# Base rows written in place by ScalarE, x and bias added to them by accumulating DMAs, most of them behind the return of the attention rows

## The reference, cut to what matters

```
x = x + gnn(xn, edges) + mix(xn)          # first residual
x = x + ffn(layernorm(x))                 # second residual, FP4-rounded weights and rows
gnn: rms scale, W_down (1024 to 256), xl = x@Wl, xr = x@Wr, per edge a LeakyReLU score,
     a softmax over the edges of each receiver, sum of alpha * xl[src], then @ W_up (256 to 1024)
mix: q, k, v = xn@W + b;  (q k^T) v * scale;  @Wo + bo      # no softmax in it
ffn: gate, up (1024 to 512), silu(gate) * up, down (512 to 1024)
```

## Time and profile before

| | us |
|---|---|
| median of 3 runs | 917.87 (916.38 to 919.6) |
| the profiled execution, its own time | 920.16 |
| its span, first to last instruction | 918.4 |
| PE busy | 856.0 (93%) |
| DVE busy | 817.6 (89%) |
| ACT busy | 549.5 (60%) |
| POOL busy | 498.9 (54%) |
| mean granted TensorE clock | 0.968 of full speed |

### The profile page before, as it was taken

The page is one execution under the profiler, slowest core; times in us unless marked ns, Lnnn a source line. Parts: engine busy times, 40 slices in busy tenths (PEclk is TensorE's granted clock), DMA queues, the critical chain, the costliest instruction groups (busy, mean ns, idle before and its releaser), DMA issues.

```text
span 918.4 us, 9530 instructions
## 1 busy us (share of the span) xinstructions
PE 856.0 (93%) x2734; PEld 417.5 (45%) x2734; DVE 817.6 (89%) x987; ACT 549.5 (60%) x1947; POOL 498.9 (54%) x528
## 2 busy tenths in 40 slices
PE   4999999999999999999999999997999699999665
PEld 3885455644444444444444444432444244444222
DVE  7989988779999999999999999999994277999994
ACT  3313123356767887779898988798995332353432
POOL 5200748578667777777777787877775200010011
PEclk9999999999999999999999999997999899999877
DMA  9322625563655333663345633349959911113125
GB/s 306 98 95 52 179 85 178 143 196 99 84 162 184 97 89 89 193 202 107 102 122 172 193 97 100 91 111 190 382 111 204 207 49 46 69 24 69 24 46 87
DMA packets 72403, 117.85 MB, mean 128 GB/s; under 512 B 29383, under 2 KB 42340, under 8 KB 72330
## 3 DMA queue, kind: packets, MB, share of 16 engines
q0 software_dynamic: 27520, 63.68, 30.2%
q1 hardware_dynamic: 44826, 53.52, 18.6%
HBM read 89.15 MB, written 17.17 MB: 116 GB/s over the span
## 4 chain that ended last, share of the span: by engine, by line
DVE 61%; PE 14%; issue 9%; POOL 8%; DMA 6%; ACT 1%; ACTq 0%; SPq 0%; POOLq 0%; DVEq 0%
DVE acc_sb L1487 12%; DVE turned L1479 11%; DVE z L1639 11%; DVE turned L1637 10%; PE acc L745 3%; POOL round_mem L550 3%; PE turned L900 2%; DMA round_mem<-msg_table,idx 2%; PE acc L933 2%; DMA acc_sb<-gnn_dram 2%; PE acc L900 2%; PE turned L955 1%; POOL round_mem L628 1%; POOL perm_dram L599 1%; POOL xr_sb L632 1%
## 5 line engine op out<-in xcount | busy, mean ns | idle before, releaser
L550 POOL DMA_INDIRECT round_mem<-msg_table,idx x352 | 345.5, 982 | 99.5 <-issue 80.0
L1122 ACT ACTIVATE round_mem<-round_mem,pz 128x65 f32<-128x65 f32 x1408 | 354.1, 398 | 7.0 <-DVE acc_sb L1487 3.0
L745 PE MATMUL acc<-wslot,big_a 128*128 128x512 f32 x512 | 220.3, 592 | 0.0
L745 PEld LDWEIGHTS acc<-wslot,big_a 128*128 128x128 f32 x512 | 97.1, 190 | 121.5 <-issue 121.3
L1487 DVE TENSOR_REDUCE acc_sb<-round_mem 128x260 f32<-128x1820 f32 (+1 forms) x62 | 121.6, 1962 | 7.2 <-ACT round_mem L1122 5.1
L1479 DVE TENSOR_TENSOR turned<-round_mem,turned 128x1560 f32<-128x1560 f32 (+1 forms) x62 | 105.4, 1700 | 7.4 <-DMA round_mem<-msg_table,idx 5.4
L1112 ACT ACTIVATE pz<-z 128x7 f32<-128x7 f32 (+1 forms) x248 | 55.4, 296 | 93.7 <-DVE z L1644 93.6
L745 PE MATMUL acc<-big_b,wslot 128*128 128x512 f32 x256 | 110.1, 592 | 0.2 <-ACT big_b L1058 0.2
L745 PE MATMUL acc<-wslot,big_b 128*128 128x512 f32 x256 | 110.0, 592 | 0.0
L1639 DVE TENSOR_REDUCE z<-turned 128x24 f32<-128x1560 f32 (+1 forms) x62 | 105.1, 1695 | 2.1
L1637 DVE SCALAR_TENSOR_TENSOR turned<-turned,att_sb 128x1536 f32<-128x1536 f32 (+1 forms) x62 | 103.6, 1671 | 0.0
(11 more groups left out here) (231 smaller groups left out, 1045.4 us busy)
## 6 DMA issues: line engine op xcount, KB each, us to landing
round_mem<-msg_table,idx POOLq DMA_INDIRECT x352, 2.8
big_b<-in_x SPq DMA_DIRECT2D x9, 512.0 KB, 7.7
big_b<-big_b SPq DMA_DIRECT2D x9, 512.0 KB, 13.2
big_b<-in_x POOLq DMA_DIRECT2D x9, 512.0 KB, 12.8
out_x<-big_b SPq DMA_DIRECT2D x9, 512.0 KB, 3.2
out_x<-acc_sb POOLq DMA_DIRECT2D x9, 512.0 KB, 5.4
wslot<-in_wv_t SPq DMA_DIRECT2D x2, 2048.0 KB, 9.3
wslot<-in_wk_t SPq DMA_DIRECT2D x2, 2048.0 KB, 9.5
```

What stands on the lines that cost most here:

```text
L550: pool.indirect_dma_start(xg[g % 4][:, j, :], None, msg_table, bass.IndirectOffsetOnAxis(idx[:, c, j0 + j:j0 + j + 1], 0)).then_inc(xg_in[ ...
L745: mm = nc.tensor.matmul(o(acc[:, n % 4, :]), a, b, start=first, stop=last)
L1122: ins = nc.scalar.activation(to[:, :, j], xg[g % 4][:, j, h * HR + 1:(h + 1) * HR], ACT.Copy, scale=pz[:, g % 2, j, h:h + 1])
```

## The change

The early base products are no longer laid aside. ACT copies each half straight from PSUM into the rows of the residual, and POOL then adds x and the bias row to them with accumulating DMAs. The order of the products is (0,0), (1,0), (0,1), (1,1), then (2,0), (2,1) and so on as before. For chunks 6 to 8, SP reads x straight into the rows, and only the bias is added. Of the sixteen accumulating DMAs, six (x of chunks 0 to 2, bias of 0 to 2) stand between POOL's last three rescalings, and ten (x of 3 to 5, bias of 3 to 8, x of 9) stand behind a wait for `gnn_in[1]`. Since x of chunk 9 is added to the place in which the bias row lies, it waits for all nine bias additions.

```diff
-BIAS_SUMS_AT, X_AT = 40, 61
+BIAS_SUMS_AT, AHEAD = 40, 3
+BETWEEN = {-2: {"x": (0, 1, 2), "bias": ()}, -1: {"x": (), "bias": (0, 1)}, 0: {"x": (), "bias": (2,)}}
...
-         "base": [(c, h) for c in range(EARLY) for h in range(2)]}
+         "base": [(c, h) for h in range(2) for c in range(2)] + [(c, h) for c in range(2, EARLY) for h in range(2)]}
...
-            sp.wait_ge(acc_taken["dve"], taken[index_of["bias", 1]])
-            for c in range(C - 1):
-                sp.dma_start(base[:, c, :], bias_bc).then_inc(x_in[c], 16)
+            sp.wait_ge(acc_full, index_of["bias", 1] + 1)
+            for c in range(EARLY, C - 1):
+                sp.dma_start(base[:, c, :], x[c * NC:(c + 1) * NC, :]).then_inc(x_in[c], 16)
...
             def add_x(c):
                 n = rows(c)
-                if c < C - 1:
-                    pool.wait_ge(x_in[c], 32)
+                if c < EARLY:
+                    pool.wait_ge(acc_taken["act"], taken[index_of["base", ORDER["base"].index((c, 1))]])
                 else:
                     for i in range(C - 1):
-                        pool.wait_ge(x_in[i], 32)
-                pool.dma_start(base[0:n, c, :], x[c * NC:c * NC + n, :], accum_op=ALU.add).then_inc(x_added[c], 16)
-
-            def lay_base(c):
-                pool.wait_ge(acc_taken["act"], taken[index_of["base", ORDER["base"].index((c, 1))]])
-                pool.wait_ge(x_added[c], 16)
-                pool.dma_start(base[:, c, :].rearrange("p (k n) -> p k n", k=KB), base_at[c], accum_op=ALU.add).then_inc(base_added[c], 16)
+                        pool.wait_ge(bias_added[i], 16)
+                pool.dma_start(base[0:n, c, :], x[c * NC:c * NC + n, :], accum_op=ALU.add).then_inc(x_added[min(c, EARLY)], 16)
+
+            def add_bias(c):
+                if c < EARLY:
+                    pool.wait_ge(x_added[c], 16)
+                else:
+                    pool.wait_ge(x_in[c], 32)
+                pool.wait_ge(acc_taken["dve"], taken[index_of["bias", 1]])
+                pool.dma_start(base[:, c, :], bias_bc, accum_op=ALU.add).then_inc(bias_added[c], 16)
...
-                if X_AT <= g < X_AT + C - 1:
-                    add_x(g - X_AT)
             for g in range(LAST - 2, LAST + 1):
+                for c in BETWEEN[g - LAST]["x"]:
+                    add_x(c)
+                for c in BETWEEN[g - LAST]["bias"]:
+                    add_bias(c)
                 rescale(g)
-                if g == LAST - 2:
-                    for c in range(max(LAST + 1 - X_AT, 0), C):
-                        add_x(c)
             for c in range(C):
                 if LAST_OF[c] + 5 > LAST:
                     send_attention(c)
-            for c in range(EARLY):
-                lay_base(c)
+            pool.wait_ge(gnn_in[1], 16)
+            for c in range(AHEAD, EARLY):
+                add_x(c)
+            for c in range(AHEAD, C - 1):
+                add_bias(c)
+            add_x(C - 1)
...
                 elif kind == "base":
                     c, h = ORDER["base"][i]
-                    act.wait_ge(acc_full, index_of["base", ORDER["base"].index((c, 1))] + 1)
-                    nc.scalar.copy(base_at[c][:, 4 * h:4 * h + 4, :], a.rearrange("p (k n) -> p k n", k=4)).then_inc(t, 1)
+                    nc.scalar.copy(base[:, c, h * HALF:(h + 1) * HALF], a).then_inc(t, 1)
...
             def residual(c, h):
-                    if c < EARLY:
-                        dve.wait_ge(base_added[c], 16)
+                    if c < C - 1:
+                        dve.wait_ge(bias_added[c], 16)
                     else:
-                        dve.wait_ge(x_added[c], 16)
+                        dve.wait_ge(x_added[EARLY], 16)
```

More of the change, by code:

```diff
@@ L223, in gps_layer @@
         x_in = [sem(f"x_in{c}") for c in range(C)]
-        x_added = [sem(f"x_added{c}") for c in range(C)]
-        base_added = [sem(f"base_added{c}") for c in range(EARLY)]
+        x_added = [sem(f"x_added{c}") for c in (*range(EARLY), C - 1)]
+        bias_added = [sem(f"bias_added{c}") for c in range(C - 1)]
         wd_in, rms_in, wlr_in = sem("wd_in"), sem("rms_in"), sem("wlr_in")
@@ L299, in gps_layer @@
                for i in range(2)]
-        base_at = [xhat_t[:, :, c * NC:(c + 1) * NC] for c in range(C)]
         gnn_tr = xr_sb[:, :, :].rearrange("p c f -> p (c f)")[:, 0:2 * NP].rearrange("p (k n) -> p k n", k=2)
@@ L883, in _ @@
                 c, h = ORDER["base"][i]
-                if i in (0, 1):
+                if i in (0, 2):
                     pe.wait_ge(acc_taken["act"], taken[index_of["t2", 7 if i == 0 else 15]])
@@ L985, in gps_layer @@
                 round_of[n], at = g, full
-                if kind == "base" and ORDER["base"][i][1] == 1:
-                    round_of[index_of["base", ORDER["base"].index((ORDER["base"][i][0], 0))]] = g
                 begun += TAKE_STEP if engine == "dve" else 0.0
@@ L993, in gps_layer @@
         for n in range(n, len(groups)):
-            kind, i, _ = groups[n]
             round_of[n] = LAST + 1
-            if kind == "base" and ORDER["base"][i][1] == 1:
-                round_of[index_of["base", ORDER["base"].index((ORDER["base"][i][0], 0))]] = LAST + 1
         def due(engine, g):
@@ L1614, in sum_p0 @@
                 ins.then_inc(p0_summed, 1)
-            assert round_of[index_of["bias", 1]] + 3 < X_AT
             def sum_bias(k):
```

## The result

The changed kernel took 933.98 us (median of 4 runs, 933.21 to 934.01). The kernel before took 918.15 us in 4 runs (916.38 to 919.6). The ratio is 1.0177, with a 95% interval of 1.0158 to 1.0196: the change makes the kernel 1.8% slower, 15.8 us. The forecast was 933 us. The profiled execution has a span of 931.7 us (before 918.4) and took 933.97 us itself, so the two profiled executions are only 13.8 us apart, because the profiled execution of before (920.16 us) was slower than all four of these. In the sixth and the seventh experiment one execution (1833.37 and 929.76 us) stood far off from the others: it is in their medians, not in their ratios.

A forecast was written before the change was run, and what follows sets the result against it. Rounds end on DVE and ACT, queued accumulations stretch the return, then PE is the chain. Root 13.1 us later plus 1.8 us of clock gives +14.9 us, the return's 12.3 spent on waiting: 933 us, range 926 to 939.

The forecast's parts named there:

- ACT's copies: In the rounds: twelve same-size copies, one at a time instead of in pairs, hidden behind DVE; 0, bounds -1 and +1 us.
- SP's bias copies: In the rounds: nine bias copies become three copies of x; at most 0.45 us to be had, value 0.
- the six early additions: Between POOL's last rescalings: their waits end before DVE needs the rescaling; value 0, with 2.6 us of cover.
- The return: Second reading-back of attention rows after the last sending: lands in 5.5 us, at 714.5 instead of 726.8, 12.3 us earlier.
- The ten additions: On POOL behind the return: chunk 0's root waits for all nine biases and ends at 743.8, 13.1 us later.
- The disputed price: Cost of each queued bias addition behind the return: taken as 2.48 us, bounds 1.31 and 2.90.
- The rivals with a cheaper bias: Additions behind the return at plain-copy pace: bias only, about 926 us (12 in 100); all accumulations, about 922 (6 in 100).
- the quoted rule: Trainium skill's DMA estimate, 1.2 us per further 512 KB: root ends about 731.3, sum near +3 us, time about 921.
- The chain through ACT to PE: At the tail's head: late root delays ACT's normalising and attention rows 6 and 7; PE starts 4.4 us after root's end.
- The clock: PE after its idle time, inside its first tail matmuls: lower clock loses 1.8 us, bounds 0 and 4.
- Nothing behind gives time back: In the tail after PE's delayed start: the chain has no fixed date, so nothing of the 14.9 us is recovered.
- last rival: At POOL's first root: if ready with ACT's deviation, the early return moves everything up some 10 us, about 908 (4 in 100).

The follow-up runs named there:

- sixth: The kernel with roots between the additions (908.2 us), but without POOL's wait for the return: 911.74 us, ratio 0.9941 to the kernel before.
- seventh experiment: The changed kernel with all ten additions behind the return, and POOL's wait for it, left out: 907.21 us, ratio 0.9882 to the kernel before.
- fifth experiment: The changed kernel without the bias additions for chunks 6, 7 and 8: 925.6 us, ratio 1.0088 to the kernel before.
- first two experiments: Changed kernel with x of chunk 9 added behind three roots: 919.76 us; changed kernel with ACT taking attention rows 6 and 7 before normalising chunk 0: 926.36 us.
- first experiment: The changed kernel with x of chunk 9, and its wait for nine biases, behind POOL's first three roots: 919.76 us, ratio 1.0022.
- third experiment: The changed kernel with roots of chunks 0 and 1 between the bias additions and x of chunk 9 behind the third root: 908.22 us, ratio 0.9893.
- fourth experiment: The changed kernel without POOL's wait for the return, x of chunks 3 and 4 issued right behind the sending: 931.15 us, ratio 1.015.

## Why the prediction was right

The forecast was 933 us with a range of 926 to 939, measured 933.98. Its steps, between the two profiled executions:

- *ACT's copies, SP's bias copies, the six early additions (0).* From DVE's first sum of the rounds to its last, 501.1 us before and 500.4 now, so 0.7 us were won, within the bounds of 1 us. I did not separate by whom. The rounds also began 0.7 us earlier (200.4 instead of 201.1), so that the last sending started 1.4 us earlier, at 704.00. The rescaling of round 60 ended at 691.15, ahead of DVE's need at 693.90.
- *The return (12.3 us earlier).* Against the last sending it is 8.46 us (704.00 to 712.46) instead of 21.4: 12.9 us earlier. The sending landed in 2.5 instead of the 3.2 I took, the reading-back in 5.5 as taken.
- *The ten additions (the root 13.1 us later).* From the last sending to the root's end it is 39.1 us now, and it was 25.3 before: 13.8 us later. The disputed price, 2.48 us for a bias addition, was right: the fifth experiment gave 2.48 again. The last of them land within 1.38 MB of traffic at 94.1% of the 16 engines. The rivals with a cheaper bias are out, and with them what the quoted rule gave for the end of the root (731.3).
- *The chain through ACT to PE.* Right. PE began L906 4.0 us behind the root's end (4.4 before), and the first two experiments cut the chain at both ends.
- *The clock (1.8 us).* The mis-sized term, within its bounds: 2.6 us (9.64 against 7.03), behind 21.9 us of idle time. It did not grow with the idle time here: behind the 9.71 us of the first experiment it was 2.9 (9.92 against 7.03).
- *Nothing behind gives time back.* At one of DVE's block maxima of the tail (L1247, at 846.94 before and 861.52 now) the two executions are 14.6 us apart, at the end 13.3. The last 71.45 us of before took 70.16 us. The same stretch took 68.0 to 71.7 us in other kernels of this study, so I take this for scatter in the end of the tail, where PE's mean clock is 0.79 in both, and not for the change.

Put together, between the two profiled executions: 1.4 us earlier, 13.8 later, 0.4 less from the root to PE, 2.6 for the clock, which makes 14.6, and 1.3 less behind it. So the path and the wait were right, and that the sum of 14.9 us comes within a microsecond of the time is in part luck: the root and the clock were taken 1.5 us too short together, and what the rounds and the end of the tail took off was taken as 0. The 14.9 lies between the 13.3 of the spans and the 15.8 of the medians.

The prediction counted the win of the return as "all spent on waiting", and in the change as written it is. Its last rival named what would keep it, a root that comes when ACT's deviation is ready, and gave about 908 us for it. The third experiment makes just that and took 908.22.

The traffic at the end of the additions, 733.5 to 741 us in the changed kernel (to be read beside the earlier trace rows):

```profile
DMA packets 386, 1.38 MB, mean 185 GB/s; under 512 B 48, under 2 KB 48, under 8 KB 386
...
q0 software_dynamic: 386, 1.38, 94.1%
```

## What to carry to other kernels

When DMAs are moved behind an event, look at what stands behind them on the issuing engine. Here a wait for the landing of the last bias, whose rows DVE first reads at 840.23, some 100 us later, held back a 0.6 us instruction for which three engines stood idle some 22 us each. An addition that must wait for others belongs as late as its own reader allows, and small instructions that others wait for go between the issues. Order first, then traffic: between the worst and the best order of the same additions lie 26 us (933.98 and 908.22), and against the kernel without them the best order costs nothing that was measured.

## What the runs showed of the hardware

- An accumulating DMA from SBUF with rows of 4 KB runs at the pace of one from HBM: 2.48 us for each 512 KB (fifth experiment), while the nine plain copies from the same source ran, beside gathers, in traffic of 399 GB/s.
- SP's transfers land later beside POOL's accumulations. The reading-back of 1024 KB landed in 5.5 us alone, and in 14.0 (before), 11.5 (fourth experiment) and 15.0 us (sixth) beside accumulations. SP's two stores of 512 KB that were issued at 717.77 and 722.08 in the changed kernel took 8.0 and 9.0 us to land. The median of nine such stores in the seventh experiment, which has no additions there, is 2.7.
